# Unused products in TensorE's gaps, and scores moved ahead of place products, in a one-core audio tower

## The reference, cut to what matters

```python
h = relu(patches(x) @ W1 + b1) @ W2 + b2
h = h + bitlinear_o(attention(bitlinear_q(n(h)), bitlinear_k(n(h)), bitlinear_v(n(h))))   # 16 heads, 32 keys
h = h + top1_experts(n(h))        # 8 experts of capacity 100: gate * (x @ w_expert + b), kept if place <= 100
h = h + state_space_filter(n(h))  # a decaying complex filter along the 32 positions
h = h + top2_mixture(n(h))        # silu(x @ W1[e]) * (x @ W2[e]) @ W3[e], two experts of 8 for each token
```

## Time and profile before

| | us |
|---|---|
| median of three runs | 514.07 |
| lowest, highest | 512.21, 514.18 |
| the profiled execution, its own time | 512.82 |
| its span, first to last instruction | 511.0 |

### The profile page before, as it was taken

The page is one execution under the profiler, slowest core; times in us unless marked ns, Lnnn a source line. Parts: engine busy times, 40 slices in busy tenths (PEclk is TensorE's granted clock), DMA queues, the critical chain, the costliest instruction groups (busy, mean ns, idle before and its releaser), DMA issues.

```text
span 511.0 us, 9246 instructions
## 1 busy us (share of the span) xinstructions
PE 434.7 (85%) x3339; PEld 278.8 (55%) x3340; DVE 288.4 (56%) x841; ACT 206.0 (40%) x385; POOL 163.0 (32%) x140
## 2 busy tenths in 40 slices
PE   0599999798767664778789999999999999999991
PEld 0245556456464553645456666676666666566661
DVE  0598978686769989999995568347411111111110
ACT  1224643463477333325435642444233233233230
POOL 6051010010101213542235446352545442554322
PEclk9999999999868876899899999999999999999998
DMA  9999210037037100553013413152323225323311
GB/s 176 253 211 206 44 42 3 9 115 252 13 92 273 36 12 1 185 193 118 10 43 82 78 28 51 33 125 32 51 42 48 53 42 185 51 51 51 42 21 21
DMA packets 36102, 43.14 MB, mean 84 GB/s; under 512 B 5216, under 2 KB 30560, under 8 KB 35904
## 3 DMA queue, kind: packets, MB, share of 16 engines
q1 hardware_dynamic: 26384, 32.14, 22.5%
q0 software_dynamic: 7488, 10.23, 12.8%
q10 hardware_dynamic: 2192, 0.27, 0.5%
HBM read 30.96 MB, written 11.53 MB: 83 GB/s over the span
## 4 chain that ended last, share of the span: by engine, by line
PE 66%; DVE 19%; issue 5%; ACT 4%; DMA 4%; SPq 1%; POOLq 0%; DVEq 0%; ACTq 0%
PE psum L2252 26%; PE psum L2271 13%; PE psum L1874 8%; PE psum L2262 3%; DMA KT<-in_L_attn_w_o_dram 3%; PE psum L1900 2%; PE psum L1888 2%; PE psum L2242 2%; PE psum L1918 2%; DVE st_att L1032 1%; PE psum L2011 1%; PE psum L2013 1%; DVE H L1274 1%; DVE M2s L907 1%; DVE Eb L1072 1%
## 5 line engine op out<-in xcount | busy, mean ns | idle before, releaser
L1774 DVE TENSOR_TENSOR QT<-QT,psum 128x512 f32<-128x512 f32 x39 | 26.8, 687 | 137.2 <-PE psum L2252 137.1
L1874 PE MATMUL psum<-M2s,M1s 128*128 128x512 f32 x128 | 61.8, 629 | 19.5 <-DMA M1s<-in_L_tok_W_dram 18.5
L2271 PE MATMUL psum<-M3s,KT 128*128 x312 | 74.1, 381 | 1.2 <-ACT KT L823 0.8
L2252 PE MATMUL psum<-M1s,KT 128*128 x156 | 74.0, 597 | 1.1 <-issue 0.6
L2252 PE MATMUL psum<-M2s,KT 128*128 x156 | 73.3, 593 | 0.0
L2271 PEld LDWEIGHTS psum<-M3s,KT 128*128 128x128 f32 x312 | 58.7, 190 | 21.9 <-issue 16.0
L834 ACT ACTIVATE O<-psum,gate_slot 128x256 f32<-128x256 f32 x39 | 18.5, 474 | 106.5 <-PE psum L2271 106.5
L504 POOL DMA_INDIRECT KT<-mixture_rows_in,src_i x39 | 41.7, 1069 | 34.2 <-issue 19.7
L2252 PEld LDWEIGHTS psum<-M2s,KT 128*128 128x128 f32 x156 | 29.7, 191 | 37.2 <-issue 37.2
L1874 PEld LDWEIGHTS psum<-M2s,M1s 128*128 128x128 f32 x128 | 24.2, 199 | 45.0 <-issue 26.0
L531 POOL DMA_INDIRECT mixture_rows_out<-O,src_i x17 | 30.9, 1815 | 32.9 <-ACT O L834 12.3
(11 more groups left out here) (406 smaller groups left out, 736.0 us busy)
## 6 DMA issues: line engine op xcount, KB each, us to landing
M3s<-in_x_dram SPq DMA_DIRECT2D x4, 1024.0 KB, 10.5
M3s<-in_L_ffn_W_dram SPq DMA_DIRECT2D x1, 4096.0 KB, 14.3
M2s<-in_L_ffn_W_dram SPq DMA_DIRECT2D x1, 4096.0 KB, 16.3
M1s<-in_L_ffn_W_dram SPq DMA_DIRECT2D x1, 4096.0 KB, 13.9
M3s<-in_x_dram SPq DMA_DIRECT2D x4, 992.0 KB, 14.2
M1s<-vtok SPq DMA_DIRECT2D x64, 34.0 KB, 1.9
mixture_rows_out<-H SPq DMA_DIRECT2D x4, 512.0 KB, 4.7
M1s<-in_L_tok_W_dram SPq DMA_DIRECT2D x2, 512.0 KB, 14.0
```

What stands on the lines that cost most here:

```text
L1774: v.tensor_tensor(sil[:, u, :], sil[:, u, :], bank[3], ALU.mult).then_inc(v_gated, 1)
L1874: last = mm(bank[6 + c], W1s[:, r, P * c:P * (c + 1)], xr[:, i % 2, r].rearrange("p b l -> p (b l)"), start=(n == 0), stop=(n == STRIDE - 1))
L2252: last = mm(z, xrT[:, u, c, :], w[:, bass.ds(e, 1), c, :].rearrange("p a h -> p (a h)"), start=(c == 0), stop=(c == CH - 1))
L2271: last = mm(bank[6][:, 0:DM], actT[:, u, c, :], M3s[:, bass.ds(e, 1), c, :].rearrange("p a d -> p (a d)"), start=(c == 0), stop=(c == HC - 1))
```

## The change

Four places get `keep_busy` (its definition moves up in the code, which shifts the line numbers behind it by 5 to 10): five products ahead of `qkv(2, 3)` in slot 3, six ahead of the scores in slot 4, six ahead of `att_mean(2)` in slot 4, and four ahead of `slot_tables(0)`, the first row numbers. In slots 4 and 5 the first half of the scores moves ahead of `places0`. No other engine's program changes.

```diff
--- before.py
+++ after.py
@@ -1856,6 +1856,11 @@
         def _(pe):
             mm = nc.tensor.matmul
             tr = nc.tensor.transpose
+            def keep_busy(n, z):
+
+                for _ in range(n):
+                    mm(z, ident_b[:], bias3[:].rearrange("p a d -> p (a d)"), start=True, stop=True)
+
             def layer1(i, c, lo=0, hi=STRIDE):
                 if c == 0 and lo == 0:
                     if i == 0:
@@ -2105,6 +2110,7 @@
             pe.wait_ge(v_att_added, 1)
             layer2(3)
             values(1, 3, range(2, BT))
+            keep_busy(5, bank[0])
             qkv(2, 3)
             wait(pe, v_less_max, BT * done(3, C_LAG))
             norm2_columns(0)
@@ -2120,10 +2126,12 @@
                     places0(iN, bank[6])
                 if iB is not None:
                     batch_mean_in(iB, slot)
+                    keep_busy(6, bank[0])
+                if iC is not None:
+                    scores(iC, slot, range(0, 2))
                 if iN is not None and (iN <= 1):
                     places0(iN, bank[6])
                 if iC is not None:
-                    scores(iC, slot, range(0, 2))
                     scores(iC, slot, range(2, BT))
                 if iD is not None:
                     att_columns(iD)
@@ -2149,6 +2157,8 @@
                     norm2_columns(iD)
                     expert_rows(iD, range(0, 1))
                     if iC == 2:
+                        pe.wait_ge(a_expert, TS * iD)
+                        keep_busy(6, bank[7])
                         pe.wait_ge(v_att_rows, 3)
                         att_mean(2)
                     expert_rows(iD, range(1, TS))
@@ -2186,11 +2196,6 @@
                                   gate_table[n][:, k, t].rearrange("p w a -> p (w a)"),
                                   start=(t == 0 and k == 0), stop=(t == tiles - 1 and k == 1))
                 last.then_inc(p_gate_table, 1)
-
-            def keep_busy(n, z):
-
-                for _ in range(n):
-                    mm(z, ident_b[:], bias3[:].rearrange("p a d -> p (a d)"), start=True, stop=True)
 
             last = STEPS - 1
             pe.wait_ge(v_att_rows, STEPS)
@@ -2222,6 +2227,7 @@
             pe.wait_ge(v_att_added, STEPS)
             keep_busy(4, bank[6])
             expert_rows(last, range(0, 1))
+            keep_busy(4, bank[7])
             slot_tables(0, EARLY, FULL_EARLY, bank[3])
             expert_rows(last, range(1, TS))
             pe.wait_ge(a_norm2T, STEPS)
```

## The result

The changed kernel takes 509.20 us in the median of 8 runs (508.77 to 511.92), the kernel before 512.97 in 8 runs on the same chip (511.04 to 515.26). The ratio is 0.9937, with a 95% interval of 0.9916 to 0.9958: 3.2 us less, with 2.2 to 4.3 in the interval (the two medians are 3.8 apart). The profiled execution took 510.68 us with a span of 508.9, so it is one of the three slower ones of the eight. The span is the time from the first to the last instruction; the rest of the time, mostly 1.8 us, lies around it.

The account below looks back on a forecast made before the run. Before the mixture, VectorE's work and TensorE at 1.2 GHz where somebody waits were taken to cost time. Terms (a) to (e) sum to 4.3 us off the profiled 512.82, giving 508.5; median forecast 509.0, range 507.0 to 512.4.

Parts of the forecast that it names:

- (a): Slot 3, five fillers ahead of the q, k, v products: clock held, 0.9 us gained; at worst 0.3 lost.
- (b): Slot 4, six fillers ahead of the scores: their first half at full clock, 1.3 us gained; at worst 0.4 lost.
- (c): Six fillers ahead of the mean of step 2: faster expert rows, 0.4 us gained; at worst 0.8 lost.
- (d): Slot 5, scores ahead of the place products: VectorE's 1.5 us wait goes, whatever the clock; bounds 1.1 to 1.6.
- (e): Four fillers ahead of the first row numbers: 0.2 us gained; bounds 0 and 0.3.
- Rival B: The clock's fall moves to the expert rows of step 0, only 2.1 us gained, 510.7 us; chance 0.12.
- rival A: Fillers too few to decide the clock in the gaps; only (d) stays, 511.2 us; chance 0.18.

Follow-up runs that it names:

- the kernel with the bridge: Changed kernel plus six more keep_busy products behind the last expert rows, ahead of the wait for the first slot's fetched rows; 508.60 us, again 509.08.

## Why the prediction was right, point by point

- The sum. The terms (a) to (d) were forecast at 0.9 + 1.3 + 0.4 + 1.5 = 4.1 us. Between the two profiles VectorE's stretch is 108.92 - 104.46 = 4.46 shorter: 0.85 for (a), 1.38 for (b), 0.39 for (c), 1.5 for (d) with 0.17 for a shorter pair of row maxima, and 0.17 that I assign to nothing. The mixture's transposes started at 250.95, where 251 to 251.5 was forecast. One of the signs for "right" didn't hold: from there to the end it takes 257.95 us in the first profile and not the 255.7 of before, since the first mixture products are slow; in the second profile of the changed kernel it is 255.4, in the third 256.2.
- Term (e), forecast as a gain of 0.2. The step that held is that the fetched rows set the start: from the second half of the row numbers to the transposes it is 255.30 - 250.15 = 5.15 us before and 250.95 - 245.78 = 5.17 after. What I didn't draw from it is that expert rows which finish sooner leave a gap of 1.7 us there, behind which the clock can be down. In the first profile the start was 1.38 us longer than before, in the other two (23.01) 0.3 shorter. Behind such a gap (1.6 to 1.8 us) the first mixture products are slow in three of eight profiles: the changed kernel's first, the fillers alone, and the second of the kernel before, which has no (e). So the fall isn't the doing of (e) alone, and what (e) is worth no run shows: without it the time is the same within the spread.
- The lower bound of (d). With the scores wholly at half clock from 179.7 on, their second set is there at 179.7 + 3.25 = 182.95, and the second row maximum ends at some 183.6, against 184.28 before. That is 0.6 gained, not the 1.1 of the bound. No profile has slow scores behind the move, so it wasn't tried.
- The share of the terms. I took the terms as independent and read each from one execution. The move alone gives a ratio of 0.9946, the fillers alone one of 0.9983, whose interval holds no change, and both 0.9937. So most of the gain is the move's. It takes away a wait of 1.5 us where the scores of slot 5 are at full clock in the old order and of 2.7 to 4.0 where they aren't, and it also closes the gap ahead of them. That (d) doesn't depend on the clock was wrong in this sense. The fillers add, beside the move, some 0.5 to 1 us in the median (1.25 in the span, where both were timed in one series), not the 2.6 of (a) to (c). Some of the falls that they are to prevent aren't in every execution of the kernel before: its second profile has q, k, v at full clock. Rival B (the fall moves) fits the profile of the fillers alone, though at the scores of slot 5 and not at the expert rows of step 0.
- The gaps. Falls stand behind gaps of 1.7 to 2.4 us in several profiles here, but the move alone shows full clock behind a gap of 1.95 us, so such a gap allows a fall and doesn't force it. The rule of the Trainium skill named in the prediction ("TensorE: Matmul & The Clock Gate", section "Why this matters for your kernels") warns only of longer gaps than these. The falls here disagree with reading it as a promise that shorter ones are free.
- The time. 509.0 was forecast and 509.2 measured. The forecast took 4.3 us off an execution 1.25 below the median then known and put 0.5 back on; the median fell by 3.0 to 3.8 in the three comparisons. The agreement to 0.2 is better than the reasons for it. The time alone doesn't speak for the forecast against rival A either: A was priced at 511.2, but the kernel without the fillers, the move alone, took 510.22. What speaks for it is the clock at the filled places and the comparison with the kernel without (e). The medians of the spans fell by 4.4 and 3.5 us (511.5 to 507.1, 510.75 to 507.3) in the two later comparisons, near the sum of 4.3. The times fell less, since 9 of the changed kernel's 23 executions have 2.5 to 2.9 us around the span.

## What to carry to other kernels

An instruction that waits for another engine should not stand in front of work that this engine is waiting for: moving the scores past the wait for the mask gave most of the gain, and the scores then also had no idle gap ahead of them, behind which the clock could be down. Unused products help only where somebody waits for the product behind the gap, and filling one gap can lengthen the next; look there before counting the gain. Where the clock's falls stand in other places from one execution to the next, take a second profile before pricing them.

## What the runs showed of the hardware

The kernel before had its falls of TensorE's clock in other places in two profiles of the same program, and the same idle gap of 1.95 us was followed by half clock in one kernel and by full clock in another. Five or more unused products in such gaps had the clock up nearly everywhere (the tables above); two did not for the scores of slot 4 (0.51). Beside that, the time around the span is 1.7 or 1.8 us in all 72 executions of the kernel before that were timed beside the experiments, but 2.5 to 2.9 in 9 of 23 of the changed kernel, 0 of 12 of the move alone and 0 of 13 of the kernel with the bridge. No run shows its cause.
